# Seven block products for eight in the gate product of four token groups

## What is computed

```python
x = x + xattn(layernorm(x), ctx, Wq, Wkv)
# feed-forward on h = layernorm(x)
h = act_qdq(h)                                # 16-bit grid, scale from the maximum over all tokens
up = act_qdq(h @ lpbq_dequant(w_up).T)        # 512 -> 1536; weights on a 4-bit grid per block of 32
gate = act_qdq(h @ lpbq_dequant(w_gate).T)    # 512 -> 1536
sig = fixed_qdq_u16(sigmoid(gate))
gate = act_qdq(gate * sig)
o = act_qdq(gate * up)
x = x + o @ lpbq_dequant(w_down).T            # 1536 -> 512
```

## Time and profile before

| | us |
|---|---|
| median of 3 runs | 903.41 |
| the runs | 898.75, 903.41, 904.83 |
| span of the profiled execution | 898.3 |
| gate product on TensorE | 130.1 to 380.6 |
| up product on TensorE | 380.5 to 631.7 |
| down product on TensorE | 640.0 to 895.0 |

### The profile page before, as it was taken

One profiled execution on the slowest core, in us unless ns is written; L12 is line 12 of the kernel. 1 busy time (PEld: TensorE's weight loads), 2 busy tenths in 40 slices (PEclk: granted clock), 3 DMA queues, 4 the chain that ended last, 5 costly groups with the idle time before them and its releaser, 6 DMA issues.

```text
span 898.3 us, 11791 instructions
## 1 busy us (share of the span) xinstructions
PE 865.5 (96%) x4144; PEld 426.7 (47%) x4144; DVE 651.1 (72%) x918; ACT 560.2 (62%) x673; POOL 157.4 (18%) x160
## 2 busy tenths in 40 slices
PE   7999969999999999999999989999799989999998
PEld 5777544444444444444444434444344434444443
DVE  4879883754346243279997859856999997999892
ACT  2378875553553454489997859763789975555430
POOL 0099940089001950000000000000000000000000
PEclk9999989999999999999999999999999999999999
DMA  9822319775369649884339993799998897989872
GB/s 347 332 93 98 128 59 305 205 194 198 140 234 296 206 161 294 322 319 157 132 149 327 363 347 142 251 402 373 374 379 265 276 322 271 386 286 406 317 294 100
DMA packets 107548, 230.20 MB, mean 256 GB/s; under 512 B 47216, under 2 KB 47216, under 8 KB 105328
## 3 DMA queue, kind: packets, MB, share of 16 engines
q1 hardware_dynamic: 106352, 225.48, 70.8%
q10 hardware_dynamic: 1152, 4.19, 1.3%
HBM read 127.40 MB, written 92.27 MB: 245 GB/s over the span
## 4 chain that ended last, share of the span: by engine, by line
PE 66%; DVE 16%; issue 8%; DMA 6%; ACT 3%; SPq 0%; POOL 0%; DVEq 0%; ACTq 0%
PE ps L871 28%; PE ps L948 13%; PE ps L903 10%; PE ps L975 3%; DVE big L1596 3%; PE ps L804 3%; DVE big L1589 3%; PE ps L743 2%; PE ps L818 2%; DVE small L1523 2%; DMA big<-gate_park 2%; DMA product_park<-big 2%; DVE small L1511 2%; DVE big L1518 1%; PE ps L965 1%
## 5 line engine op out<-in xcount | busy, mean ns | idle before, releaser
L993 ACT ACTIVATE big<-ps 128x1024 f32<-128x1024 f32 (+2 forms) x166 | 138.7, 845 | 189.6 <-PE ps L871 102.8
L871 PE MATMUL ps<-big 128*128 (+1 forms) x1152 | 250.5, 381 | 2.3 <-DVE big L1460 2.3
L903 PE MATMUL ps<-big 128*128 (+1 forms) x1152 | 249.0, 379 | 2.3 <-ACT big L993 2.3
L871 PEld LDWEIGHTS ps<-big 128*128 128x128 f16 x1152 | 113.1, 98 | 139.4 <-issue 4.6
L903 PEld LDWEIGHTS ps<-big 128*128 128x128 f16 x1152 | 112.6, 98 | 138.5 <-issue 2.8
L1478 DVE TENSOR_REDUCE small<-big 128x1 f32<-128x1024 f32 x48 | 58.3, 1219 | 135.2 <-ACT big L993 135.1
L948 PE MATMUL ps<-big 128*128 128x512 f16 x576 | 125.1, 379 | 2.7 <-DVE big L1617 2.7
L683 POOL PARTITION_ALL_REDUCE small<-small x8 | 3.3, 410 | 509.3 <-DVE small L1558 181.5
L948 PEld LDWEIGHTS ps<-big 128*128 128x128 f16 x576 | 56.2, 98 | 71.1 <-issue 2.9
L929 PE MATMUL ps<-big 128*128 128x512 f16 x384 | 85.2, 383 | 4.5 <-ACT big L1223 4.5
L1529 DVE CUSTOM_DVE_ANT_0 big<-big,small 128x1024 f32<-128x1024 int16 x48 | 61.7, 1284 | 7.3 <-ACT big L1173 0.5
(11 more groups left out here) (101 smaller groups left out, 1008.9 us busy)
## 6 DMA issues: line engine op xcount, KB each, us to landing
big<-up_park SPq DMA_DIRECT2D x90, 512.0 KB, 6.5
up_park<-big SPq DMA_DIRECT2D x48, 512.0 KB, 3.9
gate_park<-big SPq DMA_DIRECT2D x42, 512.0 KB, 2.9
big<-gate_park SPq DMA_DIRECT2D x42, 512.0 KB, 5.7
sign_park<-big SPq DMA_DIRECT2D x48, 256.0 KB, 3.1
big<-in_x_dram SPq DMA_DIRECT2D x8, 1024.0 KB, 17.5
x_park<-big SPq DMA_DIRECT2D x8, 1024.0 KB, 3.9
product_park<-big SPq DMA_DIRECT2D x16, 512.0 KB, 5.8
```

The lines of the kernel that those rows point to most:

```text
L871: mm = nc.tensor.matmul(ps[:, 2 * (n % 2) + j], w[:, a, k, o:o + P], XT[:, g, b, k], start=(k == 0 and a + b == 0), stop=(k == KC - 1 and ...
L903: mm = nc.tensor.matmul(ps[:, b + j], WU[:, a, k, o:o + P], XT[:, g, c, k], start=(k == 0 and a + c == 0), stop=(k == KC - 1 and c == 1))
L993: return nc.scalar.activation(dst, src, ACT.Copy)
```

## The change

The last four groups of the gate product are taken as two pairs. A pair's product for one unit is a 2 x 2 by 2 x 2 block product: inputs in two halves of 256 (k 0, 1 and k 2, 3), features in two blocks of 128, tokens in two groups. Instead of eight products of halves (six matmuls each, 48), the program forms seven (42) from sums of blocks, and adds and subtracts the results. One such unit is a quad; there are 12. The first four groups remain as they were, 24 "flat" units (`FLAT`).

What moves with it:

- Four sums of gate weight blocks: ten additions on POOL (`first_sums`, `last_sum`), split by ScalarE and VectorE (`sum_hi`, `sum_lo`, 1536 columns). Four sums of tokens for each pair: `turn_raw` on VectorE, `turn_hi` on ScalarE, `turn_lo` on VectorE, 1024 columns each.
- The flat units use three pairs of banks and three output slots, in place of two. The first part of h is made by ScalarE (`split_hi`, 2048 columns), not VectorE. All seven groups must be ready before the first quad.
- In a quad ScalarE copies four of the partial results from PSUM, VectorE makes four half tiles (512 columns) with one addition each (`combine`), and a maximum for each; ScalarE makes four half signs. SP stores four halves and four half signs. Each half has one slot.
- The down weights come first, in four pieces within the flat units (`DOWN_AT`, `PARK_AT`), each turned and parked by itself; the up weights are loaded in four quarters after the flat units, with rows of 512 bytes, and are split and turned in quads 6 to 10.
- No gate tile stays on chip at the end: all 48 are stored and fetched. Tile 0 is fetched in quad 10, 1 to 7 after the last product, the others during the up product (`next_gates`).
- The down weights lie in another order in DRAM and on chip, with runs of 128 values.

```diff
-        gate_out = part(HT0, 2048).rearrange("p (s w) -> p s w", s=2)
+        gate_out = [part(at, UW) for at in (HT0 + 3 * UW, HT0, HT0 + UW)]
+        gate_half = part(HT0, 2048).rearrange("p (s w) -> p s w", s=4)
+SUM_AT = (8, 10, 13, 16)
+SPLIT_AT = (3, 5, 7, 9, 11, 15, 17)
+DOWN_AT = (14, 16, 19, 21)
+PARK_AT = (16, 18, 21, 23)
+TURN_AT = (18, 12)
+UP_AT = (6, 7, 8, 9)
...
+            def quad(q):
+                base, pr, n = 4 * ((q + 1) % 2), q // UPG, q % UPG
+                g, T = pair_group(pr), turns(pr)
+                need(pe, c_ev, C_EV + 4 * (q - 1) if q > 1 else 0)
+                six(base, n, WG[:, 0], XT[:, g, :, 0:2], True)
+                if n == 0:
+                    pe.wait_ge(s_lo, S_LO + 4)
+                    pe.wait_ge(t_lo, T_LO + 4 * PAIRS)
+                    pe.wait_ge(g_ev, FLAT)
+                six(base + 3, n, SUMS[:, 0], T[:, 0], True)
+                six(base + 2, n, WG[:, 2], T[:, 3], True)
+                pe.wait_ge(c_ev, C_EV + 4 * q + 1)
+                six(base, n, SUMS[:, 1], T[:, 2], False)
+                pe.wait_ge(copy_ev, COPY_EV + 4 * q + 2)
+                six(base + 3, n, SUMS[:, 2], XT[:, g + 1, :, 2:4], False)
+                if q + 1 < QUADS:
+                    first_of(q + 1, 4 - base)
+                pe.wait_ge(copy_ev, COPY_EV + 4 * q + 4)
+                six(base, n, SUMS[:, 3], T[:, 1], False)
...
+            for u in range(FLAT):
+                act.wait_ge(g_mm, u + 1)
+                need(act, g_mx, u - 2)
...
+                if u >= 3:
+                    act.wait_ge(g_st[u % 3], 16 * (u // 3))
+                copy(gate_out[u % 3], unit_banks(u).rearrange("p b w -> p (b w)")).then_inc(g_ev, 1)
+                if u % 2 and u < 2 * NG - 3:
+                    h_int((u + 3) // 2)
+                if u in SPLIT_AT:
+                    split_hi(SPLIT_AT.index(u) + 1)
...
+            def combine(q, x, bank, other, op):
+                if q:
+                    dve.wait_ge(c_st[x], C_ST + 16 * q)
+                    dve.wait_ge(c_sign, C_SIGN + 4 * (q - 1) + x + 1)
+                else:
+                    dve.wait_ge(g_st[1 + x // 2], 16 * FLAT // 3)
+                    dve.wait_ge(g_mx, FLAT)
+                    dve.wait_ge(sign_ev, FLAT)
+                nc.vector.tensor_tensor(gate_half[:, x], ps[:, bank], other, op).then_inc(c_ev, 1)
...
+            def load_up_weights(k):
+                sp.dma_start(WN.rearrange("p (k c d) -> p k c d", k=KC, c=OC)[:, k],
+                             wu_in[:, k * P:(k + 1) * P].rearrange("(c p) d -> p c d", p=P)).then_inc(up_ld[k], 16)
```

More of the change, by code:

```diff
@@ L884, in gate, with six, first_of @@
                     pe.wait_ge(hlo_d, g + KC)
-                product(WG, g, g_mm, g_ev)
+                for n in range(UPG):
+                    need(pe, g_ev, g * UPG + n - 2)
+                    if isinstance(g, int) and g == 0:
+                        pe.wait_ge(wt_lo, (low_count(1), low_count(8), OC, OC, OC, OC)[n])
+                    flat_unit(g, n)
+            def six(bank, n, w, x, begin):
+                for k in range(2):
+                    for a, b in ((0, 0), (1, 0), (0, 1)):
+                        mm = nc.tensor.matmul(ps[:, bank], w[:, a, k, n * P:(n + 1) * P], x[:, b, k],
+                                              start=(begin and k + a + b == 0), stop=(k + b == 2), skip_group_check=True)
+                mm.then_inc(q_mm, 1)
+            def first_of(q, base):
+                g = pair_group(q // UPG)
+                six(base + 1, q % UPG, WG[:, 1], XT[:, g, :, 2:4], True)
+            def quad(q):
[17 more added lines that the diff above has]
+                six(base, n, SUMS[:, 3], T[:, 1], False)
             def keep_warm(count, square, width, bank):
@@ L892, in _ @@
             gate(0)
-            with nc.tensor.Fori(1, NG) as g:
+            with nc.tensor.Fori(1, FLAT_G) as g:
                 gate(g)
-            pe.wait_ge(wu_turned, 16 * (2 * KC + H_ODD))
+            for g in range(FLAT_G, NG):
+                pe.wait_ge(hlo_d, g + KC)
+            first_of(0, 4)
+            for q in range(QUADS):
+                quad(q)
+            pe.wait_ge(wu_turned, 16 * 2 * KC)
             def raise_unit(g, n):
@@ L947, in down_whole @@
                                 o = Qf[:, HALF[whole(q)], at] if a else hi_place(q)[:, at]
[L948 removed]
+                                mm = nc.tensor.matmul(bank_of(i), o, WD[:, b, :, 2 * n + c], start=(n == 0 and c + a + b == 0),
                                                       stop=(n == UPG - 1 and c + a == 2))
@@ new lines, in _ @@
+            act.wait_ge(q_mm, Q_MM + done_p2(0))
+            copy_out(copy_b, 5)
+            act.wait_ge(g_st[0], 16 * FLAT // 3)
+            act.wait_ge(g_mx, FLAT - 2)
+            for q in range(QUADS):
+                base = 4 * ((q + 1) % 2)
+                if q:
+                    half_sign(q - 1, 2)
+                    half_sign(q - 1, 3)
+                act.wait_ge(q_mm, Q_MM + done_p5(q))
+                need(act, c_ev, C_EV + 4 * q if q else 0)
+                copy_out(copy_d, base + 3)
+                half_sign(q, 0)
+                act.wait_ge(q_mm, Q_MM + done_p4(q))
+                copy_out(copy_c, base + 2, 4.0)
+                if q in UP_AT:
+                    natural_hi(1, 3 * UP_AT.index(q))
+                act.wait_ge(q_mm, Q_MM + done_p6(q))
+                copy_out(copy_u, base)
+                if q in UP_AT:
+                    natural_hi(1, 3 * UP_AT.index(q) + 1)
+                    natural_hi(1, 3 * UP_AT.index(q) + 2)
+                half_sign(q, 1)
+                if q + 1 < QUADS:
+                    act.wait_ge(q_mm, Q_MM + done_p2(q + 1))
+                    act.wait_ge(c_ev, C_EV + 4 * q + 2)
+                    copy_out(copy_b, 4 - base + 1)
@@ new lines, in ints, with turn_raw @@
+            def ints(g, h):
+                return hx[:, g % 2, h * 1024:h * 1024 + 1024]
+            def turn_raw(pr, j):
+                g = pair_group(pr)
+                first = (ints(g + 1, 0), ints(g + 1, 1), raw_sum[:, 1], raw_sum[:, 0])[j]
+                second = (ints(g, 0), ints(g + 1, 0), ints(g, 0), ints(g, 1))[j]
+                if j > 1:
+                    dve.wait_ge(t_raw, T_RAW + (j if pr else 4 + j))
+                    dve.wait_ge(t_lo, T_LO + (j - 1 if pr else 4 + j - 1))
+                elif pr == 0:
+                    dve.wait_ge(t_lo, T_LO + 4)
+                    dve.wait_ge(wd_turned, 32)
+                nc.vector.tensor_tensor(raw_sum[:, j % 2], first, second,
+                                        ALU.add if j == 2 else ALU.subtract).then_inc(t_raw, 1)
```

606 lines of the change are left out of this document (399 added, 207 removed).

## The result

The changed kernel takes 907.58 us (median of 6 runs, 906.45 to 910.88), the kernel before 903.22 (6 runs, 898.75 to 904.83): a ratio of 1.0064, 95% interval 1.0039 to 1.0089. So it is slower, by less than 1%. 72 matmuls are gone, and more time than they were worth was lost elsewhere. The profiled execution took 906.45 us with a span of 904.7.

The account below looks back on a forecast made before the run. TensorE, busy 96% of the span, was taken to bound the kernel. Terms: -15.5 + 7 + 3.5 + 5.5 + 1.3 + 1.5 + 0.3 = +3.6 us, giving a 907 us median; range 892 to 917 for 8 in 10.

Parts of the forecast that it names:

- Saving: Gate product: 72 matmuls fewer over 12 quads, at 0.216 us each, 15.5 us saved.
- (a): Flat units 11 to 19: nearly full VectorE and ScalarE wait on each other, copies lag, TensorE waits about 7 us.
- contention rival: Two-input VectorE instructions in the flat units all stretch beside POOL's quantizing, 4 us more: 911 us; chance 0.10.
- (b): Into the first quad: its first combination waits for late flat signs and unit 22's store, 3.5 us of TensorE wait.
- (c): Second quad: combination 0 waits for the first quad's half tile store, issued behind weight loads on SP, 5.5 us.
- So it queues: Second quad: the half tile store waits behind up-weight quarters (5.7 us) and down weights (2.85 us), partly hidden by slack.
- (d): Quads 2 and 3: VectorE's block maxima and scales bring 10.7 us of work against a quad's 9.07, 1.3 us wait.
- (e): Clock: after the waits in flat units and first two quads, matmuls run at the lower level, 1.5 us lost.
- (f): Work said to cost nothing: POOL's sums, down weights ended by about unit 16, up weights, added stores and loads.
- (g): Last stage's start: loads of down weights, now with 512-byte rows in DRAM, cost 0.3 us.
- fast rival: Flat units and first quads: ScalarE, VectorE and queues keep pace, waits shrink, 893.7 us; chance 0.20.
- rival of the slow loads: Second quad: an up-weight quarter takes over 4.5 us, its wait grows to 13, the next quad waits: 918 us; chance 0.17.

Follow-up runs that it names:

- both repairs: Changed kernel with the last two h groups' transposes at units 13 and 14 and up-weight loads spread over the quads: 899.22 us, 0.9961 of the kernel before.

## Why the prediction was right, and where only by luck

The forecast was 907, the measurement 907.6. That it came so close is luck. The sum forecast +3.6 us; the terms as measured below add up to +6.1 (-15.6, 8.1, 2.7, 7.7, 0, 2.1 and 1.1), and the profiled spans differ by 6.4. The forecast then added the 5.1 us that lie between the span and the median before; in the changed kernel they are 2.9 (904.7 and 907.6). The two errors, 2.5 to 2.8 and 2.2 us, nearly cancel. The range, the places of the three waits and the engines behind them were right by more than luck; half the cause of the first and the cause of the last were not. Term by term:

- **Saving, -15.5.** Right: 1080 gate matmuls (576 and 504), 15.6 at the pace of before. The run with as many matmuls given back bears out the price, outside of the waits.
- **(a) Flat units, 7.** 8.1 measured, at the place and with the releaser that were forecast. But the working was right for half its reason. It laid out the token sums and weight splits at their lengths alone, as the run with GpSimd quiet has them, and that run shows 2.2 us. The sharing, in the prediction a rival worth 4 us more, is what brings it from 2.2 to 8.1. The chain overestimated the rest by 5 us; the bound "2.5 without the late transposes" was 3.6, sharing included, and 0 without the sharing. What the Trainium skill says (GPSIMD Engine Reference, Specifications), that VectorE's instructions with two SBUF inputs contend with GpSimd, is what the trace shows: from 0.69 to 1.6 us and from 1.2 to 1.9 us for those, 1.20 to 1.22 throughout for the maximum. It deserved a place in the sum. The contention rival had the mechanism, and the wrong addition: it put its 4 us on top of a chain that was too long.
- **(b) First quad, 3.5.** 2.7 (0.58 behind ScalarE and 2.13 behind VectorE, which waited 3.03 us for a store of the flat part).
- **(c) Second quad, 5.5.** 7.7, the right place and releaser. The step that failed is "So it queues", behind what SP issued ahead of it. With the loads on another engine's queue, and mostly issued after it, the store still took 9.7 us; with long rows the idle was 5.97; with the loads spread it was gone. It is bytes in flight, 3 MB of loads that meet the transposes, parked weights and bunched stores of the late flat units. The lag (a) adds to it: without a lag the idle was 4.85. Both bounds named the wrong things, overtaking and short rows; the second, 13, is refuted by the long rows.
- **(d) Quads 2 and 3, 1.3.** No idle. VectorE works without a break from 296.65 to 310.8 us, and TensorE never waits for it: it has products in hand between combinations, which the term left out.
- **(e) Clock, 1.5.** 2.1 behind 7.68 us of idle, nothing behind the others in this profile. In other runs the 24 matmuls of the last flat unit took 6.7 to 7.0 us instead of 5.35, behind idles of 2.2 to 3.7 us, so the length of the idle alone doesn't tell.
- **(f) At nothing.** Right for the time, wrong for GpSimd's pace. GpSimd ended the down weights at 239.5 us (unit 21) instead of unit 16; its sums took 3.1 us each, its own instructions were stretched too (from 1.48 to 2.3 us and more). Nobody waited for it, but its longer work lay beside VectorE's for longer. The up weights (318.85 to 359.9) cost nothing, as said.
- **(g) 0.3.** The rest of the span, from the up product on, is 1.1 us longer: the up product's idle 0.5 (2.84, before 2.29), the down product's idle 0.8 (5.3, before 4.5), a little less elsewhere.

The fast rival's premise, that queues keep pace, can be bought: both repairs together gave 899.2, not 893.7. The rival of the slow loads did not decide: a quarter took 8 us to land, beyond the 4.5 that the rival named, yet not from short rows, and no second wait followed.

## What to carry to other kernels

Before a matmul is traded for vector work, add up VectorE's and ScalarE's work per unit of TensorE's pace, with two-input VectorE instructions at their length beside GpSimd wherever GpSimd works at the same time. Here 45.7 us of work in 46.6 us of matmuls, counted without that, did not fit. A single-slot buffer makes the landing time of its store part of the loop, so big loads belong behind that store, one at a time, and another queue doesn't help; the DMA share doesn't show the difference. Time gained ahead of a stage need not arrive at the end: of 11.0 us here, 3.3 were given back in the up product, for a reason that stays open.

## What was not expected of the hardware

- A DMA issue can hold its engine: 4.93 us on SP and 7.65 us (two loads) on ScalarE behind quarter loads of 1536 pieces of 512 bytes, 0.46 us for the same store behind loads of 128 pieces.
- Sharing is mutual: GpSimd's products of 768 columns went from 1.48 to 2.3 to 3.0 us beside VectorE, its additions of a constant from 0.83 to 1.7 or 2.2.
- In the up product, the last 432 matmuls took 93.4 to 93.5 us behind an idle of 2.29 or 2.84 us (three kernels), and 94.9 to 95.9 behind 3.41 to 5.02 us (nine kernels; in a tenth, behind 3.60 us, nothing was lost): one more microsecond of wait went with up to 2.5 us more in the matmuls.
